# Narrow window attention on Trainium2: the inverse norms of a tile as one power on GpSimd, where VectorE took Newton steps

## What is computed

```python
def l2norm(t):
    return t / jnp.maximum(jnp.linalg.norm(t, axis=-1, keepdims=True), 1e-12)

q, k, v = split(x @ Wqkv, 3)            # 16 heads of 64 channels
q = l2norm(q) * qs;  k = l2norm(k) * ksc
q = q * cos * scale + rotate_half(q) * sin * scale
k = k * cos / scale + rotate_half(k) * sin / scale
out = local_attention(q, k, v)          # softmax over the own and the previous window of 32
```

## Time and profile before

| what | value |
|---|---|
| time, median of 3 runs | 8041.49 us (8037.83 to 8042.28) |
| time of the profiled execution | 8054.26 us |
| span of its trace, first to last instruction | 8052.5 us |
| mean granted TensorE clock over the span | 0.903 of full speed |
| HBM traffic over the span | 217.42 MB read, 42.14 MB written, 32 GB/s |

### The profile page before, as it was taken

The page is one execution under the profiler, slowest core; times in us unless marked ns, Lnnn a source line. Parts: engine busy times, 40 slices in busy tenths (PEclk is TensorE's granted clock), DMA queues, the critical chain, the costliest instruction groups (busy, mean ns, idle before and its releaser), DMA issues. The chain is left out here.

```text
span 8052.5 us, 245024 instructions
## 1 busy us (share of the span) xinstructions
PE 6439.7 (80%) x93014; PEld 4367.5 (54%) x93078; DVE 5558.3 (69%) x11704; ACT 4997.1 (62%) x10684; POOL 4334.9 (54%) x3786
## 2 busy tenths in 40 slices
PE   5776999999999999999998599977888667733377
PEld 2334666666666666666665488874555423322355
DVE  6895777777777777777777477766666668854432
ACT  5545888888888888888887344436766555402022
POOL 5775666666666666666665245544444367731000
PEclk8888999999999999999999799998999878866588
DMA  3322112112112111112111200001010133232001
GB/s 125 123 113 63 47 47 60 48 47 60 48 46 58 50 46 55 53 45 60 49 48 36 75 6 6 6 19 28 22 29 22 36 141 130 99 113 77 23 0 31
DMA packets 344469, 440.84 MB, mean 55 GB/s; under 512 B 151976, under 2 KB 235648, under 8 KB 324416
## 3 DMA queue, kind: packets, MB, share of 16 engines
q1 hardware_dynamic: 335632, 405.19, 16.3%
q10 hardware_dynamic: 1584, 15.21, 0.5%
q0 software_dynamic: 6144, 5.25, 0.4%
HBM read 217.42 MB, written 42.14 MB: 32 GB/s over the span
## 5 line engine op out<-in xcount | busy, mean ns | idle before, releaser
L841 POOL TENSOR_TENSOR L0f_qr<-L0f_qs,L0f_table 128x512 f32<-128x512 f32 x776 | 1008.0, 1299 | 425.4 <-ACT L0f_qs L882 349.2
L1105 PE MATMUL L0f_ring<-L0f_wqkv,L0f_hT 128*128 128x512 f32 x2324 | 1208.3, 616 | 25.2 <-DVE L0f_m L991 13.5
L914 ACT ACTIVATE L0f_prob<-L0f_scores,L0f_nmx,L0f_rn 128x64 f32<-128x64 f32 x3072 | 1013.7, 441 | 136.2 <-DVE L0f_nmx L1023 135.1
L848 POOL TENSOR_TENSOR L0f_qr<-L0f_qr,L0f_m 128x512 f32<-128x512 f32 x776 | 986.3, 1271 | 143.8 <-issue 102.4
L855 POOL TENSOR_TENSOR L0f_qr<-L0f_qr,L0f_rn 128x512 f32<-128x512 f32 x388 | 396.4, 1042 | 562.2 <-DVE L0f_rn L1014 529.5
L882 ACT ACTIVATE L0f_qs<-L0f_ring 128x512 f32<-128x512 f32 x776 | 469.9, 606 | 238.5 <-PE L0f_ring L1105 224.2
L1112 PE MATMUL L0f_ring<-const_ident,L0f_qr 128*128 128x128 f32 x3088 | 512.1, 290 | 119.1 <-POOL L0f_qr L855 107.8
L991 DVE TENSOR_TENSOR L0f_m<-L0f_ring,L0f_table 128x512 f32<-128x512 f32 x776 | 530.8, 684 | 59.5 <-ACT L0f_qs L882 28.2
L887 ACT ACTIVATE L0f_sq<-L0f_qs 128x512 f32<-128x512 f32 x776 | 494.2, 637 | 51.5 <-DVE L0f_ssq L999 10.9
L999 DVE TENSOR_REDUCE L0f_ssq<-L0f_sq 128x8 f32<-128x512 f32 x776 | 524.3, 676 | 0.4
L1105 PEld LDWEIGHTS L0f_ring<-L0f_wqkv,L0f_hT 128*128 128x128 f32 x2324 | 380.2, 197 | 185.3 <-issue 122.7
(11 more groups left out here) (537 smaller groups left out, 17300.1 us busy)
## 6 DMA issues: line engine op xcount, KB each, us to landing
L0f_vmix<-L0f_vb SPq DMA_DIRECT2D x768, 128.0 KB, 2.3
L0a_bc_all<-L0a_bc_rows SPq DMA_DIRECT2D x32, 2048.0 KB, 11.2
L2a_bc_all<-L2a_bc_rows SPq DMA_DIRECT2D x32, 2048.0 KB, 11.1
L0f_vmix<-L0f_vb SPq DMA_DIRECT2D x672, 64.0 KB, 2.0
L1f_vmix<-L1f_vb SPq DMA_DIRECT2D x96, 128.0 KB
L0f_wqkv<-L_ffn_wqkv_dram SPq DMA_DIRECT2D x7, 1536.0 KB, 6.1
L2f_parts<-L2f_zero ACTq DMA_DIRECT2D x8, 1088.0 KB, 12.1
n_s<-mixer_out SPq DMA_DIRECT2D x32, 256.0 KB, 4.9
```

Source lines behind the costliest of these rows:

```text
L841: e.tensor_tensor(rotated, qs[:, q % QN], spread(cos, 1, 8), ALU.mult).then_inc(cosed.sem, 1)
L848: e.tensor_tensor(rotated, rotated, m2[:, q % SN], ALU.add).then_inc(added.sem, 1)
L914: a = e.activation(prob[:, s, j, h * KEYS:h * KEYS + KEYS], s_ps[:, s, h, j], ACT.Exp, bias=nmx[:, s, col:col + 1], scale=rn[:, tt, 2 * u, ...
L1105: e.matmul(bank[:], hT[:, buffer_of(it, step), tt * P:tt * P + P], wqkv[:, layer % 2, col:col + 512], start=True, stop=True).then_inc(full, 1)
```

## The change

The `newton` event is taken apart. DVE keeps only the floor, which now comes directly behind the sum of squares of the tile's last chunk (delay 2.01 in place of 7.67 on the planner's clock). POOL gets a new event, `power`: one instruction that raises the 32 floored sums of each token to the power -1/2, which it reads from a tile of constants. It stands at the planner's 7.67, ahead of the two `kmul`, and is the one that now sends `normed`. In POOL's order that falls between `cos` and `add` of the next tile's first q chunk.

```diff
 # dve_events
-                found.append((D["newton"], ("newton", step[1])))
+                found.append((D["ssq"] + 0.01, ("floor", step[1])))
 # pool_events
             if step[2:] == QK_ORDER[-1]:
+                found.append((D["newton"], ("power", step[1])))
                 found += [(D["kmul"] + i, ("kmul", step[1], "k", i)) for i in range(n_chunks)]
...
-        est = r.sb("est", [P, PER_TILE, 8])
+        minus = r.sb("minus", [P, PER_TILE, 8])
...
-            normed = r.count("normed", made_by(DVE_STEPS, "newton"))
+            floored = r.count("floored", made_by(DVE_STEPS, "floor"))
+            normed = r.count("normed", made_by(POOL_STEPS, "power"))
 # POOL, once, in the BEFORE stage
+                    e.memset(minus[:], -0.5)
 # POOL's body
                             e.tensor_tensor(rotated, rotated, m2[:, q % SN], ALU.add).then_inc(added.sem, 1)
                             e.drain()
+                        elif kind == "power":
+                            tt = step[1]
+                            flat = lambda t: t.rearrange("p c h -> p (c h)")
+                            z, out = flat(ssq[:, tt % 2]), flat(rn[:, tt])
+                            e.wait_ge(*floored(it, (tt,)))
+                            e.tensor_tensor(out, z, flat(minus[:]), ALU.pow).then_inc(normed.sem, 1)
+                            e.drain()
 # DVE's body
-                        elif kind == "newton":
-                            tt = step[1]
-                            flat = lambda t: t.rearrange("p c h -> p (c h)")
-                            z, t, out = flat(ssq[:, tt % 2]), flat(est[:]), flat(rn[:, tt])
+                        elif kind == "floor":
+                            z = ssq[:, step[1] % 2]
                             e.drain()
-                            e.tensor_scalar(z, z, 1e-24, None, ALU.max)
-                            e.drain()
-                            e.tensor_scalar(out.bitcast(I32), z.bitcast(I32), -0.5, float(0x5F3759DF), ALU.mult, ALU.add)
-                            for i in range(3):
-                                e.drain()
-                                e.scalar_tensor_tensor(t, out, -0.5, out, ALU.mult, ALU.mult)
-                                e.drain()
-                                e.tensor_tensor(t, t, z, ALU.mult)
-                                e.drain()
-                                a = e.scalar_tensor_tensor(out, t, 1.5, out, ALU.add, ALU.mult)
-                            a.then_inc(normed.sem, 1)
+                            e.tensor_scalar(z, z, 1e-24, None, ALU.max).then_inc(floored.sem, 1)
```

More of the change, by code:

```diff
@@ L586, in programs @@
             for _, tt, what, c in QK:
-                assert place["ssq", tt, what, c] < place["newton", tt]
+                assert place["ssq", tt, what, c] < place["floor", tt]
+                assert what == "q" or place["power", tt] < place["kmul", tt, what, c]
                 assert place["cos", tt, what, c] < place["add", tt, what, c]
```

## The result

The changed kernel takes 8339.9 us (median of 4 runs, 8329.3 to 8352.2); the kernel before, on the same chip, 8040.0 us. The ratio is 1.0374, with a 95% interval of 1.0356 to 1.0391: **slower by 300 us**. The forecast was 8500 us, slower by 450, in a range from 8000 to 8850.

The account below looks back on a forecast made before the run. PE sets the pace before; POOL was to become the bound. Per tile 21.7 us against 19.4, over 192 tiles 442 us, with the filling stage 450, gave 8504, less 12.8 for the profiled run: 8500 us, range 8000 to 8850.

Parts of the forecast that it names:

- its own sign: Main stage: forecast wrong if the power is shorter than 5.6 us or PE's wait for `kmul` does not grow.
- rival D: POOL's power takes 2.8 to 5.6 us and its load still fits; 7990 to 8290 us, about 8080; chance 0.07.
- A: The forecast: POOL's power paid per number, port free early; 8500 us, own range 8300 to 8700; chance 0.63.
- the set-up that any such instruction has is in the 201 ns of the sum: POOL's power: the 835 ns surplus for 4 numbers is paid per number, 209 ns each, so 32 take 6.9 us.
- the forecast's own sum: POOL's order and remaining waits give 21.7 us per tile, 2.3 over 19.4; 450 us with the filling stage.
- So POOL becomes the bound: Main stage: POOL's load becomes 82.9 us per iteration, over the present 77.5, adding at least 259 us.
- DVE's 2.98 us gain ... is worth nothing: Newton steps removed from DVE save 2.98 us per tile, which lies beside POOL's tail and wins no time.
- Rival B: The power keeps DVE's second SBUF input out until it ends, delaying nmx; 8750 us; chance 0.12.
- C: The power's surplus is a fixed start, about 1.1 us; faster by about 120 us, 7920 us; chance 0.18.

Follow-up runs that it names:

- run with the multiplication: The changed kernel with the power replaced by a multiplication of the same 128x32 shape on POOL, inverse norms left out: 7817.9 us.
- the reordered run: The changed kernel with two planner delays altered, so the power and both `kmul` precede `cos` and `add` of the next tile's first chunk on POOL: 8186.9 us.
- the run with 16 powers: The changed kernel with only the 16 numbers of k raised to the power, the 16 of q multiplied instead: 7952.7 us.
- the table of four: Times with Newton on DVE or without, beside a short slot or none on POOL (8041, 7818 us) or a power of 32 (8436, 8340 us).
- the early run: The kernel before with the Newton steps on DVE directly behind the sums of squares (delay 2.01 in place of 7.67): 8760.9 us.
- the row of sizes: The changed kernel with powers, then multiplications, of 1 to 128 numbers added one by one on POOL in the first stage: 8380.6 us.

## Why the prediction was right, and where it was off

**Right: direction, place and the way to PE.** The power stands ahead of `kmul` on POOL's queue, PE's `tk0` waits for it in nearly every tile (2.06 us per tile, "over 2" was said), and the wait of `kmul` for norms is gone. The run with the multiplication shows that the power's length is the cause, and the reordered run that it acts on the way to `kmul`: 153 us come back with the same work.

**By its own sign the forecast was wrong.** It called itself wrong "if the power is shorter than 5.6 us", and the power takes 5.44. That is the case of rival D, whose range of 7990 to 8290 us the measured 8340 exceeds. POOL is busy for 86% of the stage where over 90% was said, PE for 87% and not 82%, and an iteration lasts 83.2 us and not 87. The time fell into A's own range with a power that A had wrong, so a part of the agreement is luck.

**The term that was mis-sized: the power.** It is paid per number, but 0.38 us of the 1.04 are a start; 159 ns per number make 5.44 us, not 6.9. The step "the set-up that any such instruction has is in the 201 ns of the sum" was wrong. With 5.58 us per tile, its gap included, in place of 7.08, the forecast's own sum is 21.7 - 1.5 = 20.2 us per tile, 0.8 over 19.4, some 160 us.

**"So POOL becomes the bound".** With 5.58 us per power the sum gives POOL 54.6 + 4 x 5.58 = 76.9 us per iteration, less than the 77.5 of the kernel before, and the "at least" of 259 us falls away. POOL's measured work and gaps are 78.4 of 83.2 us, which by itself would have added about 40 us in 48 iterations; most of the 270 are waits on the loop through `kmul`, as the reordered run and the run with 16 powers show. POOL's load stands right behind that loop.

**The gaps and the waits.** The rest of the sum was too low. With the power at its measured length it had 72.8 us of work per iteration, 4.2 of gaps and 4.0 of waits; measured are 72.2, 6.2 and 4.8. The gaps missed most: the sum counted those of two lines and the power, while `kmul`, which waits for nobody now, and the layer norm's steps have some too. ACT's copies still cost POOL 1.0 us per tile where I left 0.3, the layer norm's statistics 0.1 where I left 0.5. So the power was some 290 us too dear and gaps and waits some 130 us too cheap: two errors of opposite sign brought 450 near 300.

**"DVE's 2.98 us gain ... is worth nothing".** It is worth 96 us under the power, by the table of four. That DVE is idle for 890 us in the stage did not make work in the middle of its queue free. The floor, placed earlier, was to cost 0.18 to 0.48 us as before; it averages 754 ns now for 483, since it often stands beside POOL's instructions of 512 numbers.

**Rival B** is out. In the kernel after, POOL's power and two of DVE's rows from the same stretch:

```profile
2601.62 5.44 POOL L859 TENSOR_TENSOR L0f_rn<-L0f_ssq,L0f_minus 128x32 f32<-128x32 f32 x1 [0.16 <-issue]
...
2602.99 0.69 DVE L1020 TENSOR_REDUCE L0f_mx<-L0f_scores 128x8 f32<-128x512 f32 x1 [0.31 <-PE L0f_scores L1130]
2603.76 0.17 DVE L1022 SCALAR_TENSOR_TENSOR L0f_nmx<-L0f_mx,L0f_rn 128x8 f32<-128x8 f32 x1
```

The nmx at 2603.76 reads two SBUF tiles and takes 0.17 us inside the power. So do all 147 that begin inside one (166 to 182 ns); the 234 that begin beside another instruction of POOL average 803 ns. The longest takes 1.2 us, where B asked for 3, and the mean of all fell from 631 to 555 ns. By the Trainium skill, "SBUF — State Buffer", section "Who interferes with whom", the one shown would have stood until 2607.06; for the power the measurement decides against it, while the Newton steps beside `cos` and `add` (the early run) behaved as it says.

**Rivals C and D.** A fixed start of the whole surplus (C) is excluded by the row of sizes, but its other side exists: a slot of 0.25 us gave 7818, where C had 7920 for 1.1 us. D's range was too narrow at both ends: a slot of 3.1 us gave 7953, below its 7990, and the power of 5.44 us 8340, above its 8290. Between these two a straight line crosses the kernel before near 3.6 us, an estimate from the two runs; C had put that point at 2.76.

## What to carry to other kernels

Before an instruction moves to POOL, get two sizes of it from a trace or measure them: one size cannot tell a start from a price per number, and here the forecast put 580 us between the two (8500 and 7920). Count an instruction by the loop that it lies on, in both places: 3 us in the middle of DVE's queue cost 96 us, and up to 223 with what waits for them, although DVE had 24% idle, and 5.4 us on POOL cost more because the k products wait for it. A shorter computation in the same place, one Newton step fewer, won 114 us where the move lost 300.

## What the runs showed of the hardware

A power on POOL costs 0.38 us plus 159 ns per number and partition, from 1 to 128 numbers, alike on constants and in place (5.43 and 5.44 us); a multiplication of 32 numbers takes 252 ns. The power does not keep DVE's two-input instructions out: 147 nmx inside it took 166 to 182 ns. In the run with power and Newton steps together, 529 of the first lines of a Newton step began inside a power and took 191 to 196 ns. POOL's sums and products of 512 numbers do keep them out: the same line, L1010, averaged 503 ns in the early run, beside them, and 269 in the old place, where POOL mostly stood. The floor, with one SBUF input, stands beside them as well (181 ns beside an idle POOL, 928 on average beside them in the kernel after). And PE's granted clock was lower in the runs in which PE stood longer: 0.99 with two Newton steps, 0.98 before, 0.96 after the change and 0.91 in the run with early Newton steps. The same instructions took longer there: 3632 us over 48 iterations of the early run, 3423 before.
